# Two-layer gated cross-attention and MoE kernel: six weight slots in the memory of four, and four experts' weights loaded ahead of the second stage

## The reference, cut to what matters

```python
x = x + tanh(g_xattn[0]) * set_attention(layernorm(x), ctx, ...)
h = layernorm(x)                                   # 2048 rows of 512
topk_idx, topk_w = top6(sqrt(softplus(h @ gate_w.T)) + bias)
g = einsum('ech,eih->eci', xb, w_gate)             # E=32, c=192 rows, i=256, h=512
u = einsum('ech,eih->eci', xb, w_up)
yb = einsum('eci,ehi->ech', silu(g) * u, w_down)
x = x + tanh(g_ffn[0]) * (sum of the rows' weighted yb + shared expert)
x = x + tanh(g_xattn[1]) * attention(layernorm(x), ctx, ctx)      # 16 heads
x = x + tanh(g_ffn[1]) * moe_of_8(layernorm(x))                   # 8 experts, 2 per row
```

## Time and profile before

| what | us |
|---|---|
| median of 3 runs | 1208.76 |
| lowest and highest run | 1204.76, 1212.23 |
| the profiled execution's own time | 1218.6 |
| span of the profiled execution | 1216.7 |
| PE busy (share of the span) | 1056.7 (87%) |
| DVE, ACT, POOL busy | 479.6, 341.5, 386.3 |

### The profile page before, as it was taken

How to read it: one execution, slowest core, us unless ns; L and a number is a source line. 1 busy time by engine, 2 the same in 40 slices (tenths; PEclk the granted TensorE clock), 3 DMA queues, 4 the chain that set the end, 5 groups by cost and what they waited for, 6 DMA issues and landing times.

```text
span 1216.7 us, 13055 instructions
## 1 busy us (share of the span) xinstructions
PE 1056.7 (87%) x4351; PEld 705.6 (58%) x4351; DVE 479.6 (39%) x1148; ACT 341.5 (28%) x537; POOL 386.3 (32%) x340
## 2 busy tenths in 40 slices
PE   5886698979979989995599899999089999999996
PEld 4333243469869778884385657675055655565553
DVE  5678757333424544332854644515011111111110
ACT  3464141023323433332243332311012222221221
POOL 0004767525435445453002020202013332333232
PEclk9788699989989999997699999999589999999999
DMA  9111011179989998965406120209913323332330
GB/s 330 70 52 43 11 62 36 51 275 277 260 274 263 263 242 234 246 159 84 159 18 57 47 44 9 52 18 307 320 48 64 62 54 62 68 63 54 64 70 8
DMA packets 52800, 148.52 MB, mean 122 GB/s; under 512 B 12243, under 2 KB 12627, under 8 KB 47296
## 3 DMA queue, kind: packets, MB, share of 16 engines
q1 hardware_dynamic: 24752, 81.09, 21.0%
q0 software_dynamic: 24160, 44.03, 18.8%
q10 hardware_dynamic: 3824, 22.57, 5.8%
HBM read 109.76 MB, written 41.08 MB: 124 GB/s over the span
## 4 chain that ended last, share of the span: by engine, by line
PE 63%; DMA 16%; DVE 10%; issue 4%; ACT 3%; POOL 3%; ACTq 0%; SPq 0%; POOLq 0%; DVEq 0%
PE pb L561 15%; PE pb L577 8%; DMA acc_rows<-big 7%; PE pb L449 7%; PE pb L534 5%; DMA big<-hn_rows,big 5%; PE pb L308 4%; PE pb L310 4%; PE pb L309 4%; DVE big L874 4%; PE pb L315 3%; PE pb L403 3%; PE pb L371 3%; POOL acc_rows L1284 2%; DMA list_rows<-big 2%
## 5 line engine op out<-in xcount | busy, mean ns | idle before, releaser
L561 PE MATMUL pb<-big 128*128 x624 | 193.2, 463 | 4.1 <-issue 4.1
L449 PE MATMUL pb<-big 128*128 128x192 f32 x1024 | 174.1, 329 | 2.1 <-ACT bigr L721 1.3
L449 PEld LDWEIGHTS pb<-big 128*128 128x128 f32 x1024 | 169.8, 192 | 6.4 <-issue 3.4
L561 PEld LDWEIGHTS pb<-big 128*128 128x128 f32 x624 | 116.6, 192 | 63.4 <-issue 6.2
L1253 POOL DMA_INDIRECT list_rows<-big x96 | 95.8, 998 | 137.2 <-DVE big L886 108.5
L1284 POOL DMA_INDIRECT acc_rows<-big x64 | 95.4, 1491 | 138.2 <-DMA acc_rows<-big 53.5
L308 PE MATMUL pb<-bigr 128*128 128x512 f32 (+2 forms) x320 | 132.9, 415 | 7.0 <-DVE big L882 4.6
L1311 POOL DMA_INDIRECT out<-big x39 | 61.8, 1584 | 207.4 <-ACT big L854 207.4
L310 PE MATMUL pb<-bigr 128*128 128x512 f32 (+2 forms) x320 | 127.6, 399 | 0.0
L309 PE MATMUL pb<-bigr 128*128 128x512 f32 (+2 forms) x320 | 127.1, 397 | 0.0
L874 DVE TENSOR_TENSOR big<-big,pb 128x352 f32<-128x352 f32 (+4 forms) x87 | 33.4, 383 | 206.5 <-ACT big L848 192.4
(11 more groups left out here) (119 smaller groups left out, 1167.8 us busy)
## 6 DMA issues: line engine op xcount, KB each, us to landing
big<-in_we SPq DMA_DIRECT2D x32, 1024.0 KB, 8.0
rawr<-in_we SPq DMA_DIRECT2D x32, 512.0 KB, 4.4
big<-in_we ACTq DMA_DIRECT2D x1, 8704.0 KB, 41.5
hn_rows<-big SPq DMA_DIRECT2D x32, 256.0 KB, 2.0
big<-in_we ACTq DMA_DIRECT2D x1, 6528.0 KB, 54.4
big<-in_x SPq DMA_DIRECT2D x4, 1024.0 KB, 15.3
acc_rows<-big SPq DMA_DIRECT2D x16, 256.0 KB, 4.2
big<-acc_rows SPq DMA_DIRECT2D x16, 256.0 KB, 4.8
```

What stands on the lines that cost most here:

```text
L449: r = e.matmul(ps[:, m * CAP:(m + 1) * CAP], WR[b % 4][:, at_:at_ + 128], XT[b % 2][:, k, :], start=(k == 0), stop=(k == 3))
L561: r = e.matmul(ps[:, 0:I1], XT1[b % 2][:, k, :], W1[:, bass.ds(r0 + (q * 4 + k) * I1, I1)], start=(k == 0), stop=(k == 3))
```

## The change: what it does, and the diff

The ring WR gets six slots of 2048 words in place of four of 3072, with six semaphores. Slots 0, 1 and 3 are loaded at the start of the first stage, and slot 2 as SP's first step after the start, when PE has used WQ, which now lies there. SW0 lies in slot 4 and the first half of slot 5, the two small arrays in the rest of slot 5. "fw" of expert n now waits for up of n-6. RD keeps three buffers; two of them move to the memory of YS, which the first stage does not use, and are loaded at the start with the down weights of experts 0 and 1. YS moves to where these two were. The wait for the end of the first stage passes from dw.0 to fw.4, which is first in SP's order of the second stage.

```diff
-SP_1 = "hn.0.0 hn.0.1 ...
+SP_1 = "fw.2 hn.0.0 hn.0.1 ...
...
+        rawd = second_name("rawd", 50432, 52480, F32)
...
-        WR = [ring(WE0) for _ in range(4)]
-        YS = [ring(D, p1=HALF) for _ in range(4)]
-        SW0 = WR[2]
-        early = taker(RING + 3 * WE0, RING + 4 * WE0)
-        WQ, DT, BQB = early(4, D), early(4, 64), early(4, 128)
+        WR = [ring(2 * D * 2) for _ in range(6)]
+        RD_AT = ring.at[0]
+        ring.at[0] += 2048
+        SW0 = S(RING + 4 * 2048, WE0)
+        WQ = S(RING + 2 * 2048, 4, D)
+        early = taker(RING + 4 * 2048 + WE0, RING + 6 * 2048)
+        DT, BQB = early(4, 64), early(4, 128)
...
-        RD = [RAW(18688 + 1024 * i, 1024) for i in range(3)]
+        RD = [rawd[:, 0:1024], rawd[:, 1024:2048], RAW(18688, 1024)]
+        YS = [S(19712 + D * i, D, p1=HALF) for i in range(4)]
...
-        l_wr = [sem(f"l_ring{i}") for i in range(4)]
+        l_wr = [sem(f"l_ring{i}") for i in range(6)]
...
-        sp2 = "dw.0 dw.1 fw.2 dw.2 fw.3 " + words(lambda n: (f"dw.{n + 3} " if n + 3 < E0 else "") + (f"fw.{n + 4}" if n + 4 < E0 else ""), E0)
+        sp2 = "fw.4 dw.2 fw.5 " + words(lambda n: (f"dw.{n + 3} " if n + 3 < E0 else "") + (f"fw.{n + 6}" if n + 6 < E0 else ""), E0)
...
-                    e.wait_ge(l_wr[b % 4], 16 * (b // 4 + 1))
+                    e.wait_ge(l_wr[b % 6], 16 * (b // 6 + 1))
...
-            for i in range(2):
-                e.dma_start(WR[i][:, 0:2048], a["we0"][i][:, 0:2048]).then_inc(l_wr[i], 16)
+            for i in (0, 1, 3):
+                e.dma_start(WR[i], a["we0"][i][:, 0:2048]).then_inc(l_wr[i], 16)
+            for i in range(2):
+                e.dma_start(RD[i], a["we0"][i][:, 2048:3072]).then_inc(l_rd[i], 16)
...
                 elif kind == "dw":
-                    if b == 0:
-                        e.wait_ge(s_pe, pe_end1)
-                        e.wait_ge(s_dve, dve_end1)
-                        stores_landed(e, l_acc)
                     if b >= 3:
                         e.wait_ge(s_dve, dv("split", b - 3))
                     e.dma_start(RD[b % 3], a["we0"][b][:, 2048:3072]).then_inc(l_rd[b % 3], 16)
                 elif kind == "fw":
-                    if b >= 4:
-                        e.wait_ge(s_pe, pe("up", b - 4))
-                    e.dma_start(WR[b % 4][:, 0:2048], a["we0"][b][:, 0:2048]).then_inc(l_wr[b % 4], 16)
+                    if b == 2:
+                        e.wait_ge(s_pe, pe("query"))
+                    if b == 4:
+                        e.wait_ge(s_pe, pe_end1)
+                        e.wait_ge(s_dve, dve_end1)
+                        stores_landed(e, l_acc)
+                    if b >= 6:
+                        e.wait_ge(s_pe, pe("up", b - 6))
+                    e.dma_start(WR[b % 6], a["we0"][b][:, 0:2048]).then_inc(l_wr[b % 6], 16)
```

More of the change, by code:

```diff
@@ L60 @@
 POOL_1 = "scatter.0 scatter.1 scatter.2 scatter.3 lists0 fetch.0 fetch.1"
-SP_1 = "hn.0.0 hn.0.1 hn.0.2 hn.0.3 hn.1.0 hn.1.1 hn.1.2 hn.1.3 hn.2.0 hn.2.1 hn.2.2 hn.2.3 hn.3.0 hn.3.1 acc.0.0 hn.3.2 hn.3.3 acc.0.1 acc.0.2 acc.0.3 acc.1.0 acc.1.1 acc.1.2 acc.1.3 acc.2.0 acc.2.1 acc.2.2 acc.2.3 acc.3.0 acc.3.1 acc.3.2 acc.3.3"
+SP_1 = "fw.2 hn.0.0 hn.0.1 hn.0.2 hn.0.3 hn.1.0 hn.1.1 hn.1.2 hn.1.3 hn.2.0 hn.2.1 hn.2.2 hn.2.3 hn.3.0 hn.3.1 acc.0.0 hn.3.2 hn.3.3 acc.0.1 acc.0.2 acc.0.3 acc.1.0 acc.1.1 acc.1.2 acc.1.3 acc.2.0 acc.2.1 acc.2.2 acc.2.3 acc.3.0 acc.3.1 acc.3.2 acc.3.3"
 PE_3 = "kflip.0 flip3.0.0 flip3.0.1 flip3.0.2 flip3.0.3 gate3.0.0 route1.0 gate3.0.1 routet1.0 up3.0.0 aflip.0 up3.0.1 gate3.0.2 ascore.0 gate3.0.3 up3.0.2 up3.0.3 gate3.0.4 gate3.0.5 pflip.0 up3.0.4 av.0 down3.0.0 kflip.1 count1.0 down3.0.1 flip3.1.0 aflip.1 flip3.1.1 down3.0.2 ascore.1 flip3.1.2 flip3.1.3 down3.0.3 route1.1 gate3.1.0 up3.1.0 up3.1.1 up3.1.2 routet1.1 pflip.1 gate3.1.1 gate3.1.2 up3.1.3 av.1 up3.1.4 count1.1 kflip.2 gate3.1.3 flip3.2.0 flip3.2.1 aflip.2 gate3.1.4 gate3.1.5 flip3.2.2 flip3.2.3 ascore.2 down3.1.0 down3.1.1 pflip.2 down3.1.2 down3.1.3 route1.2 up3.2.0 av.2 gate3.2.0 kflip.3 gate3.2.1 gate3.2.2 aflip.3 routet1.2 up3.2.1 ascore.3 count1.2 up3.2.2 gate3.2.3 gate3.2.4 up3.2.3 up3.2.4 pflip.3 gate3.2.5 av.3 down3.2.0 down3.2.1 flip3.3.0 flip3.3.1 down3.2.2 flip3.3.2 flip3.3.3 down3.2.3 gate3.3.0 gate3.3.1 up3.3.0 up3.3.1 gate3.3.2 gate3.3.3 route1.3 up3.3.2 up3.3.3 routet1.3 gate3.3.4 gate3.3.5 up3.3.4 count1.3 down3.3.0 down3.3.1 down3.3.2 down3.3.3 turnl1"
@@ L214, in program @@
         INH, INL = [R(17152, 2 * CAP), R(17536, 2 * CAP)], [R(17920, 2 * CAP), R(18304, 2 * CAP)]
-        RD = [RAW(18688 + 1024 * i, 1024) for i in range(3)]
+        assert RD_AT == 50432
+        RD = [rawd[:, 0:1024], rawd[:, 1024:2048], RAW(18688, 1024)]
+        YS = [S(19712 + D * i, D, p1=HALF) for i in range(4)]
         SLR, INR = [RAW(21760, 2 * CAP), RAW(22144, 2 * CAP)], [RAW(22528, 2 * CAP), RAW(22912, 2 * CAP)]
@@ L448, in _ @@
                                 at_ = base + k * 256 + m * 128
-                                r = e.matmul(ps[:, m * CAP:(m + 1) * CAP], WR[b % 4][:, at_:at_ + 128], XT[b % 2][:, k, :], start=(k == 0), stop=(k == 3))
+                                r = e.matmul(ps[:, m * CAP:(m + 1) * CAP], WR[b % 6][:, at_:at_ + 128], XT[b % 2][:, k, :], start=(k == 0), stop=(k == 3))
                     r.then_inc(s_pe, c.up())
```

## The result

| | executions | median us | lowest, highest |
|---|---|---|---|
| before, first comparison | 4 | 1210.49 | 1204.76, 1224.28 |
| after, first comparison | 4 | 1222.86 | 1220.39, 1226.52 |
| before, four later sessions | 121 | 1207.9 | 1186.57, 1227.06 |
| after, four later sessions | 48 | 1206.7 | 1188.40, 1217.67 |

The account below looks back on a forecast made before the run. The second stage was taken as held by the latency of POOL's transfers beside the weights, with PE close behind. Terms 0 + 1.5 + 0 + 2.5 = 4.0 us off 1208.76 gave 1204.8 us, range 1195.5 to 1211.5.

Parts of the forecast that it names:

- First stage, added loads at nothing: First stage: 3.15 MB more loads run in idle transfer time until about 45 us, cost 0; uncovered at most 8.7 us.
- first stage ends later: Sign against the forecast: the first stage's end, expected unchanged near 254 us, comes later.
- from the sum to the time: Whole kernel: 4.0 us taken from the runs' median of 1208.76 us gives 1204.8 us; range 1195.5 to 1211.5 us.
- slower by over 1%: Whole kernel above 1220.8 us, said to need an uncovered 8.7 us in the first stage together with the slower rival; chance 0.04.
- First loads, 1.5 us: Second stage's start: first burst of 2.62 MB instead of 3.67 MB saves 1.5 us, at most 9.1.
- Middle, 0: Middle of the second stage: loads come earlier, not fewer, and PE waits for none, so the gain is 0.
- End, 2.5 us: Second stage's end: weights finish about two periods earlier, so two experts run beside 512 KB instead of 1536; saves 2.5 us.
- Sum, 4.0 us: All parts together, 0 + 1.5 + 0 + 2.5, make the kernel 4.0 us faster.
- Bytes: Rival: second stage moves at DMA's pace, so 3.15 MB less saves 13.1 us, capped at 12.7: 1196.1 us; chance 0.13.
- The burst is worth nothing: Rival: the smaller burst at the second stage's start gains nothing, only the end's 2.5 us remains: 1206.3 us; chance 0.20.
- Hidden anyway: Rival: no weight is waited for, so earlier loads change nothing, and adds still hold the gathers: 1208.8 us; chance 0.13.
- Slower, because the stretch behind the shared weights goes: Rival: four periods from 356 us go at 9.91 us instead of 8.74, net 2.2 us longer: 1211.0 us; chance 0.12.

Follow-up runs that it names:

- the new places alone: Kernel before with the changed kernel's buffer places and semaphores, every load timed and ordered as before; ratio 1.0024 to the kernel before.
- loads ahead alone: Changed kernel keeping the added first-stage loads, but second-stage gate and up loads wait for up four experts earlier; ratio 1.0010, median 1205.37 us.
- fourth experiment: Changed kernel with six slots but without the added first-stage loads, so 5.77 MB is issued when the second stage begins; ratio 1.0158, median 1221.17 us.
- without weights: Changed kernel without gate and up loads of experts 6 to 31 and down loads of 3 to 31; ratio 0.9898, median 1184.89 us.

## Why the prediction was wrong, and where it was right

By the first comparison it missed by 18 us and on the wrong side. By its steps, with first-add times: "after" is the mean of five profiles of the changed kernel, "without loads ahead" that of three (the kernel before twice, the new places alone), and "ring of four" adds the kernel with loads ahead alone to these three.

- **First stage, added loads at nothing.** What was forecast of the transfers holds: done by 45 us and PE's busy time there unchanged. Up to 160 us the first profile of the changed kernel was even 1.1 us ahead of the one before. But "first stage ends later" was named as a sign against the forecast, and there it did, by 4.7 us in its first add. The later profiles have the first add at 272.6 to 273.3 us, ahead of the 274.1 and 276.3 in the two of the kernel before: not a cost of the loads.
- **The failed step** is the one from the sum to the time. I took 4.0 us off the median of three runs, and let "the runs of before spread by 4 us to each side" stand for the noise, though the profiled execution itself lay 9.8 us above that median. Over 121 executions the kernel before lies between 1186.57 and 1227.06 us. A sum of 4 us in a kernel whose executions spread by 40, with granted clocks that differ as well, needed a wider range, and more than 0.04 for slower by over 1%: nine of these 121 unchanged executions were at or above 1220.39 us. That this spread, and not the change, made the four first executions slow is argued, not shown: the later sessions exclude a lasting cost of 1.2%, but nothing reproduced a session like the first, so the cause of its 12 us stays open.
- **First loads, 1.5 us** (bounds 0 to 9.1). Experts 0 to 6 take 54.8 us after (51.8 to 58.1), against 58.0 without loads ahead (55.5 to 61.1): 3.2 us less, in the bounds and twice the size, though the spreads overlap. The fourth experiment, with a larger burst, speaks for the mechanism. The wait view of the first profile, 0.8 us at 300 to 356, looked like nearly the whole 9.1; the other four profiles have 7.7, 9.0, 5.9 and 10.1, so that fall does not stand. I sized the term by gathers' landing alone; the adds are the chain.
- **Middle, 0.** Experts 9 to 24 take 145.2 us after (140.9 to 150.8) and 142.4 without loads ahead (137.4 to 146.3). A loss of 2.8 us lies inside these spreads. With a ring of four the one profile with loads ahead took 132.9, so whether the six slots cost time in the middle stays open.
- **End, 2.5 us** (0 to 3.6). Experts 24 to 31: 54.8 us after, 57.7 with the ring of four. 2.9 us less, near the forecast, but not by the steps as I had them. I let two periods fall from 9.91 us to PE's own 8.74; the two from expert 24 to 26 take 7.4 us each after and 9.4 with the ring of four. That is below PE's own period, so adds that are late in the middle catch up here: without weights, with little to catch up, experts 24 to 31 take 56.6 us. Part of this gain then gives back what the middle lost, though how much is not shown. The waits after 500 us average 1.6 us over five profiles; below 1.5 was forecast.
- **Sum, 4.0 us.** First to last add 288.7 us after, 292.5 without loads ahead: 3.8 us, with an interval of 4.3. That it comes so near the 4.0 is luck in part: the first loads gave more than forecast, and the middle took back the difference. The pooled means differ by 2.3 us, with an interval of 2.7: the terms agree with it, and it cannot be told from nothing.

The rivals. *Bytes* (1196.1 us) fails: with 3.15 MB less in the stage, the kernel with loads ahead alone has a ratio of 1.0010, and the pooled gain of the kernel after is 2.3 us, not 12.7. But its core, that the stage is held by weights in flight, has its 20 us in the run without weights.

*The burst is worth nothing* fails by the fourth experiment, as far as that goes. Adds issued at 265 to 300 us landed in 8.3 us with the 5.77 MB burst; with 3.67 MB in 4.9, and 7.8 and 5.7 in two further profiles; with 2.62 MB in 4.4 to 6.0 over five. By the Trainium skill ("DMA: Bandwidth & Descriptors", section on queues, rings and completion order) each engine goes round its queues packet by packet. I concluded from it that the number of loads waiting would not matter. The runs do not decide against that rule: with the large burst more was also moving beside the first adds, 381 GB/s against 224, so how much waits and how much moves were not separated.

The rows of gathers that I called the nearest had compared burst with no burst on one transfer kind, of which the chain is not made. *Hidden anyway* (1208.8 us) cannot be told from the forecast by the times; the stage parts lean to the forecast, inside their spread. *Slower, because the stretch behind the shared weights goes* came true in some executions: PE's own period held for three steps, from expert 9 to 12, in the first profile, and not at all in that of the first later session (9.0, 11.9 and 10.5 us from expert 8 on); in those of the second and the fourth it holds for at least six. The kernel before has it for four steps in one profile and for thirteen in the other, so it varies without the change, and it is no lasting cost.

## What to carry to other kernels

When a serial chain of small accumulating transfers runs beside a stream of weights, look at the landing time of the chain's links, not at who waits for weights: PE waited for no weights here, and without them the kernel was some 20 us faster. More slots for prefetch need their first filling where the queue is idle; filled at the start of the busy stage they cost 1.1% here, and filled ahead they gained nothing that could be measured with POOL's order as it was. And before a difference near 1% is explained, repeat both kernels in several sessions and split a profile by stage: a change that loses its time outside the stage it touches has probably not caused the loss.

## What was not expected of the hardware

- One program took between 1186.57 and 1227.06 us over 121 executions on four chips, and run against itself gave 0.9952 with an interval that leaves out 1. Mean granted clock and time go together, -12.6 us for each 0.01.
- In the same place, with the same work and the same idle time of PE ahead of it, the granted clock was 0.50 in one execution and 0.89 in another (204 to 212 us), and eight matmuls took 5.17 us against 3.70; an execution of the unchanged kernel had 0.60 and 5.08.
- An accumulating transfer lands in 4.3 us with almost no weights beside it and in 5.9 to 7.7 us beside them (medians at 270 to 500 us). With a first burst of 5.77 MB those issued at 265 to 300 us took 8.3 us, with 2.62 MB 4.7, in one profile each.
